# A linear-attention layer with its feed-forward part: rotary and decay products moved between engines and memories

## What is computed

```python
q = rope(norm(x) @ wq.T)            # 16 heads
k, v = rope(norm(x) @ wk.T), norm(x) @ wv.T     # 4 heads, each for 4 query heads
rot = jnp.concatenate([-x2, x1], axis=-1)       # rope: x * cos + rot * sin
scores = einsum('bhid,bhjd->bhij', q, k) * diag # diag: exp(-lam * (i - j)) for i >= j, else 0
o = einsum('bhij,bhje->bhie', scores, v)        # the chunked scan of the reference gives this sum
x = x + o @ wo.T
hidden = fwht(silu(norm(x) @ W1.T) * (norm(x) @ W3.T))
x = x + hidden @ W2.T
```

## Time and profile before

| | |
|---|---|
| median of 3 runs | 289.08 us (288.9 to 290.38) |
| profiled execution, first to last instruction (span) | 287.6 us |
| PE, VectorE (DVE), ACT, GpSimd (POOL) busy | 261.9, 229.2, 164.5, 175.0 us |
| share of the span | 91, 80, 57, 61% |
| DMA | 13.23 MB, 46 GB/s in the mean |
| chain that ended last | PE 34%, DVE 34%, POOL 13%, issue 12%, ACT 4% |

### The profile page before, as it was taken

How to read it: one execution, slowest core, us unless ns; L and a number is a source line. 1 busy time by engine, 2 the same in 40 slices (tenths; PEclk the granted TensorE clock), 3 DMA queues, 4 the chain that set the end, 5 groups by cost and what they waited for, 6 DMA issues and landing times.

```text
span 287.6 us, 4155 instructions
## 1 busy us (share of the span) xinstructions
PE 261.9 (91%) x1480; PEld 226.0 (79%) x1480; DVE 229.2 (80%) x324; ACT 164.5 (57%) x271; POOL 175.0 (61%) x117
## 2 busy tenths in 40 slices
PE   0897898997997999889999979969999999999995
PEld 0685677885896888778898878859888889988885
DVE  2878999999999999876989999999667686234323
ACT  2586776669475686556668658486445453033320
POOL 1049799789975978955687897969795610000000
PEclk9999999999999999999999999999999999999999
DMA  7694020211102020000001002200000000110002
GB/s 269 228 370 135 2 74 1 73 32 43 73 2 74 5 70 1 0 2 0 1 13 63 0 2 73 74 0 2 0 2 0 0 3 0 39 36 0 2 0 73
DMA packets 5203, 13.23 MB, mean 46 GB/s; under 512 B 576, under 2 KB 2112, under 8 KB 5184
## 3 DMA queue, kind: packets, MB, share of 16 engines
q1 hardware_dynamic: 4752, 12.65, 12.4%
q10 hardware_dynamic: 432, 0.33, 0.3%
HBM read 11.93 MB, written 1.05 MB: 45 GB/s over the span
## 4 chain that ended last, share of the span: by engine, by line
PE 34%; DVE 34%; POOL 13%; issue 12%; ACT 4%; DMA 1%; DVEq 0%; SPq 0%; POOLq 0%; ACTq 0%
PE bank L264 11%; PE bank L265 11%; PE bank L266 11%; DVE p_lo L780 7%; DVE rope_b L753 6%; POOL qk L629 6%; DVE p_raw L775 5%; DVE rope_a L752 5%; POOL q_hid L636 4%; DVE xn L721 3%; DVE w_lo L727 3%; DVE o_lo L785 2%; POOL k_lo L636 2%; ACT p_hi L507 1%; DMA x_sb<-in_x 1%
## 5 line engine op out<-in xcount | busy, mean ns | idle before, releaser
L629 POOL TENSOR_TENSOR qk<-rope_a,rope_b 128x512 f32<-128x512 f32 x40 | 66.9, 1687 | 18.9 <-DVE rope_b L753 18.8
L264 PE MATMUL bank<-xt_hi,w_hi 128*128 128x512 f32 x144 | 58.5, 407 | 5.2 <-DVE rope_a L752 3.8
L265 PE MATMUL bank<-xt_lo,w_hi 128*128 128x512 f32 x144 | 57.2, 397 | 0.0
L266 PE MATMUL bank<-xt_hi,w_lo 128*128 128x512 f32 x144 | 57.1, 397 | 0.0
L636 POOL TENSOR_TENSOR q_hid<-qk,q_hid 128x512 fp32r<-128x512 f32 x32 | 48.6, 1529 | 4.0 <-ACT q_hid L500 3.9
L780 DVE TENSOR_TENSOR p_lo<-p_raw,p_hi 128x512 fp32r<-128x512 f32 x32 | 40.1, 1255 | 3.0 <-ACT p_hi L507 2.6
L507 ACT ACTIVATE p_hi<-p_raw 128x512 fp32r<-128x512 f32 x48 | 30.1, 626 | 15.4 <-DVE p_raw L775 14.8
L264 PEld LDWEIGHTS bank<-xt_hi,w_hi 128*128 128x128 f32 x144 | 27.6, 192 | 13.5 <-DVE rope_a L752 5.5
L641 POOL TENSOR_TENSOR p_lo<-p_raw,p_hi 128x512 fp32r<-128x512 f32 x16 | 25.9, 1617 | 20.2 <-ACT p_hi L507 20.1
L753 DVE TENSOR_TENSOR rope_b<-rope_b,sin_sb 128x512 f32<-128x512 f32 x40 | 36.8, 919 | 0.0
L265 PE MATMUL bank<-w_lo,o_hi 128*128 128x256 f32 x128 | 36.2, 283 | 0.0
(11 more groups left out here) (70 smaller groups left out, 611.6 us busy)
## 6 DMA issues: line engine op xcount, KB each, us to landing
w_raw<-in_w SPq DMA_DIRECT2D x6, 512.0 KB, 3.2
w_raw<-in_wq SPq DMA_DIRECT2D x4, 512.0 KB, 4.8
decay_sb<-in_decay SPq DMA_DIRECT2D x4, 512.0 KB, 5.9
w_raw<-in_wo SPq DMA_DIRECT2D x4, 512.0 KB, 3.3
x_sb<-in_x SPq DMA_DIRECT2D x4, 256.0 KB, 4.6
out<-x_sb SPq DMA_DIRECT2D x8, 128.0 KB, 1.8
w_raw<-in_wk SPq DMA_DIRECT2D x1, 512.0 KB, 4.8
w_raw<-in_wv SPq DMA_DIRECT2D x1, 512.0 KB, 6.6
```

The costliest lines, as they stand in the source:

```text
L264: pe.matmul(o, a_hi, b_hi, start=first, stop=False, skip_group_check=shared)
L265: pe.matmul(o, a_hi, b_lo, start=False, stop=False, skip_group_check=shared)
L266: return pe.matmul(o, a_lo, b_hi, start=False, stop=last, skip_group_check=shared)
L629: pool.tensor_tensor(qk[:, r % 2, :], rope_a[:, r % 2, :], rope_b[:, r % 2, :], ALU.add).then_inc(rope_sum, 1)
```

## The change

The two swap copies on ACT are removed. VectorE makes the sine product straight from the projection's bank, in two operations on 64 partitions each, which read one half of the partitions and write the other; the cosine product comes third and frees the bank. The signs of the sine table move with the partitions that are read. The decay products of S_FIRST0 and S_SECOND are written back into their PSUM bank; ACT and VectorE read them there, and PE waits for the low part before it overwrites the bank. S_FIRST1 still goes through `p_raw`, now with a buffer per unit. The low parts of chunks 3 to 13 move from VectorE to GpSimd, at the end of each unit. The order is written anew on three engines: in unit u, ACT rounds the key ahead of `o_hi` of unit u - 1, and the first query ahead of `o_hi` of unit u; GpSimd adds and splits the key at the start and the queries in the unit that projects them; VectorE rotates the key after the first low part.

```diff
...
 x_hi_done, v_hi_done = sem("x_hi_done"), sem("v_hi_done")
-swapped, rope_parts, rope_sum = sem("swapped"), sem("rope_parts"), sem("rope_sum")
+sin_done, rope_sum = sem("sin_done"), sem("rope_sum")
 rope_hi, rope_lo = sem("rope_hi"), sem("rope_lo")
...
         pe.wait_ge(rope_lo, needed + 1)
-        if u:
-            pe.wait_ge(mask_done, 3 * (u - 1) + s + 1)
+        if u and s == S_FIRST1:
+            pe.wait_ge(mask_done, 3 * u)
+        elif u:
+            pe.wait_ge(p_lo_dve, 2 * (u - 1) + s + 1)
         if s == S_SECOND:
...
         g = p // PPG
-        if b == 0:
-            pe.wait_ge(p_lo_dve, 2 * (u + 1))
-        else:
+        pe.wait_ge(p_lo_dve, 2 * (u + 1))
+        if b:
             pe.wait_ge(p_lo_pool, u + 1)
...
         if n == 1:
-            pe.wait_ge(mask_done, 3 * UNITS - 1)
+            pe.wait_ge(p_lo_dve, 2 * UNITS)
         if n >= 2:
...
-    def swap(item):
-        n, r = LIN_NO[item], ROPE_NO[item]
-        act.wait_ge(lin_full, n + 1)
-        if r >= 2:
-            act.wait_ge(rope_sum, r - 1)
-        h = P // 2
-        act.activation(rope_b[0:h, r % 2, :], lin_bank(n)[h:P], ACT.Copy)
-        act.activation(rope_b[h:P, r % 2, :], lin_bank(n)[0:h], ACT.Copy).then_inc(swapped, 1)
     def high_rope(item):
...
             act.wait_ge(o_full, 2 * u)
-        act.activation(p_hi[:, s, :], p_raw[:, n % 2, :], ACT.Copy).then_inc(p_hi_done, 1)
+        src = p_raw[:, u % 2, :] if s == S_FIRST1 else s_bank[s][:]
+        act.activation(p_hi[:, s, :], src, ACT.Copy).then_inc(p_hi_done, 1)
     def high_o(u, b):
...
                     high_v(*item[1:])
-                else:
-                    swap(item)
...
     high_weights(2)
+    high_rope(("K", 0, 0))
+    high_v(0, 0)
+    high_rope(("Q", 0, 0))
+    high_v(0, 1)
     high_weights(3)
-    swap(("K", 0, 0))
-    swap(("Q", 0, 0))
-    high_v(0, 0)
-    high_rope(("K", 0, 0))
-    swap(("Q", 0, 1))
-    high_v(0, 1)
-    high_rope(("Q", 0, 0))
-    swap(("Q", 0, 2))
+    high_rope(("Q", 0, 1))
     high_v(0, 2)
-    high_rope(("Q", 0, 1))
-    swap(("Q", 0, 3))
+    high_rope(("Q", 0, 2))
     high_v(0, 3)
-    high_rope(("Q", 0, 2))
-    high_p(0, S_FIRST0)
     high_rope(("Q", 0, 3))
-    high_p(0, S_SECOND)
     for u in range(UNITS):
-        if u:
-            before = queries(u - 1)
-            fill(key(u - 1) + turned(u - 1))
-            for item in before[:1]:
-                high_rope(item)
-            high_p(u, S_FIRST0)
-            for item in before[1:]:
-                high_rope(item)
-            high_o(u - 1, 1)
-            high_p(u, S_SECOND)
-        fill(values(u)[:2] + queries(u)[:1])
+        fill(key(u - 1) + turned(u - 1) if u else [])
+        high_p(u, S_FIRST0)
+        high_p(u, S_SECOND)
         for item in key(u - 1) if u else []:
             high_rope(item)
-        fill(queries(u)[1:])
+        if u:
+            high_o(u - 1, 1)
+        fill(values(u)[:1])
         high_p(u, S_FIRST1)
+        fill(values(u)[1:2] + queries(u))
         if u in (UNITS - 2, UNITS - 1):
...
         fill(values(u)[2:3])
+        for item in queries(u)[:1]:
+            high_rope(item)
         high_o(u, 0)
+        for item in queries(u)[1:]:
+            high_rope(item)
         fill(values(u)[3:])
...
     def rope_add(item):
         r = ROPE_NO[item]
-        pool.wait_ge(rope_parts, r + 1)
+        pool.wait_ge(lin_free, LIN_NO[item] + 1)
         if r >= 2:
...
-    def low_p(u, s):
-        n = 3 * u + s
-        pool.wait_ge(p_hi_done, n + 1)
-        pool.tensor_tensor(p_lo[:, s, :], p_raw[:, n % 2, :], p_hi[:, s, :].bitcast(F32),
+    def low_weights(n):
+        _, _, at = CHUNKS[n]
+        pool.wait_ge(w_lo_done, n)
+        pool.wait_ge(w_hi_done, n + 1)
+        pool.tensor_tensor(w_lo[:, at:at + CH], w_raw[:, n % SLOTS, :], w_hi[:, at:at + CH].bitcast(F32),
+                           ALU.subtract).then_inc(w_lo_done, 1)
+    def low_p(u):
+        pool.wait_ge(p_hi_done, 3 * (u + 1))
+        pool.tensor_tensor(p_lo[:, S_FIRST1, :], p_raw[:, u % 2, :], p_hi[:, S_FIRST1, :].bitcast(F32),
                            ALU.subtract).then_inc(p_lo_pool, 1)
...
     def butterfly(dc, step):
...
     low_rope(("Q", 0, 0))
+    rope_add(("Q", 0, 2))
     low_rope(("Q", 0, 1))
-    rope_add(("Q", 0, 2))
     rope_add(("Q", 0, 3))
     low_rope(("Q", 0, 2))
+    low_weights(3)
     low_rope(("Q", 0, 3))
     for u in range(UNITS):
-        if u:
-            before = queries(u - 1)
-            for item in before[:1]:
-                low_rope(item)
-            if u % PAIRS == 3:
-                inverse_deviation(u // PAIRS + 1)
-            for item in key(u - 1):
-                rope_add(item)
-            for item in before[1:] + key(u - 1):
-                low_rope(item)
-        low_p(u, S_FIRST1)
+        before = key(u - 1) if u else []
+        for item in before:
+            rope_add(item)
+        if u % PAIRS == 3:
+            inverse_deviation(u // PAIRS + 1)
+        for item in before:
+            low_rope(item)
+        low_p(u)
         for item in queries(u):
             rope_add(item)
+        for item in queries(u):
+            low_rope(item)
+        if unit_chunk(u) is not None:
+            low_weights(unit_chunk(u))
         if u >= UNITS - 2:
...
     def rotate(item):
...
         n, r = LIN_NO[item], ROPE_NO[item]
-        dve.wait_ge(swapped, r + 1)
+        dve.wait_ge(lin_full, n + 1)
         if r >= 2:
...
                      for m in (lin_bank(n)[:], rope_a[:, r % 2, :], rope_b[:, r % 2, :]))
-        c, s = (tb[:].unsqueeze(1).broadcast_to([P, BH, SEQ]) for tb in (cos_sb, sin_sb))
-        dve.tensor_tensor(a, src, c, ALU.mult).then_inc(lin_free, 1)
-        dve.tensor_tensor(b, b, s, ALU.mult).then_inc(rope_parts, 1)
+        h = P // 2
+        for to, at in ((slice(0, h), slice(h, P)), (slice(h, P), slice(0, h))):
+            s = sin_sb[at, :].unsqueeze(1).broadcast_to([h, BH, SEQ])
+            dve.tensor_tensor(b[to], src[at], s, ALU.mult)
+        dve.tensor_tensor(a, src, cos_sb[:].unsqueeze(1).broadcast_to([P, BH, SEQ]),
+                          ALU.mult).then_inc(lin_free, 1)
     def mask(u, s):
         c, p = divmod(u, PAIRS)
...
             dve.wait_ge(decay_loaded[p // 2], 16)
-        if s == S_FIRST1:
-            dve.wait_ge(p_lo_dve, 2 * u + 1)
-        elif u and s == S_FIRST0:
-            dve.wait_ge(p_lo_dve, 2 * u)
-        elif u:
-            dve.wait_ge(p_lo_pool, u)
+        if s == S_FIRST1 and u >= 2:
+            dve.wait_ge(p_lo_pool, u - 1)
         table = decay_sb[:, 2 * p:2 * p + 2, :]
...
             src = s_bank[s][:].rearrange("p (b h t) -> p b h t", b=BH, h=2)
-            dst = p_raw[:, n % 2, :].rearrange("p (b h t) -> p b h t", b=BH, h=2)
         else:
             src = s_bank[s][:].rearrange("p (h t) -> p h t", h=2)
-            dst = p_raw[:, n % 2, :].rearrange("p (h t) -> p h t", h=2)
+        dst = p_raw[:, u % 2, :].rearrange("p (h t) -> p h t", h=2) if s == S_FIRST1 else src
         dve.tensor_tensor(dst, src, table, ALU.mult).then_inc(mask_done, 1)
...
     def low_p(u, s):
...
         dve.wait_ge(p_hi_done, n + 1)
-        dve.tensor_tensor(p_lo[:, s, :], p_raw[:, n % 2, :], p_hi[:, s, :].bitcast(F32),
+        dve.tensor_tensor(p_lo[:, s, :], s_bank[s][:], p_hi[:, s, :].bitcast(F32),
                           ALU.subtract).then_inc(p_lo_dve, 1)
...
     def low_o(u, b):
...
-    def fill(*lists):
-        for items in lists:
-            for item in items:
-                if item[0] == "X":
-                    low_x(*item[1:])
-                elif item[0] == "V":
-                    low_v(*item[1:])
-                else:
-                    rotate(item)
+    def fill(items):
+        for item in items:
+            if item[0] == "X":
+                low_x(*item[1:])
+            elif item[0] == "V":
+                low_v(*item[1:])
+            else:
+                rotate(item)
...
     dve.wait_ge(tables_loaded, 48)
-    fill(START[2:5])
-    low_weights(3)
-    fill(START[5:])
-    mask(0, S_FIRST0)
-    mask(0, S_SECOND)
-    low_p(0, S_FIRST0)
-    low_p(0, S_SECOND)
+    fill(START[2:])
     for u in range(UNITS):
+        before = key(u - 1) if u else []
+        mask(u, S_FIRST0)
+        mask(u, S_SECOND)
+        low_p(u, S_FIRST0)
+        fill(before + turned(u - 1) if u else [])
+        low_p(u, S_SECOND)
         if u:
-            mask(u, S_FIRST0)
-            mask(u, S_SECOND)
-            fill(key(u - 1) + turned(u - 1))
-            low_p(u, S_FIRST0)
             low_o(u - 1, 1)
-            low_p(u, S_SECOND)
         fill(values(u)[:1])
...
             add_attention(0, 1)
-        fill(values(u)[1:2] + queries(u))
+        fill(values(u)[1:2])
+        fill(queries(u))
         if u in (UNITS - 2, UNITS - 1):
...
         fill(values(u)[3:])
-        if unit_chunk(u) is not None:
-            low_weights(unit_chunk(u))
         i, p = u // PAIRS + 1, u % PAIRS
...
```

(2 more changed lines are left out.)

## The result

The changed kernel takes **313.11 us** (median of four runs, 311.73 to 314.31) against 289.24 for the kernel before in the same session: a ratio of 1.0809, with a 95% interval of 1.0776 to 1.0842. The ratio is the one on record; the quotient of the two medians is 1.0825. Ratios and their intervals leave out executions in the chip's slower state, which only e13 has, in two of six, the profiled one among them. The forecast was 310.0 in a range of 289 to 318. The profiled execution spans 311.2 us, where the one before spans 287.6.

What follows compares the result with a forecast made beforehand. VectorE and PE were taken as full in the first attention units, but the time as set by queue order. 289.1 - 0.6 - 14.1 + 36.5 = 310.9, less some 0.9 for p_hi copies, gave 310; range 289 to 318.

Steps and rivals of the forecast that it cites:

- The walk: Unit-by-unit schedule of all engine queues, giving each unit's first scores and PE waits summing to 40.2 us.
- The halved price: VectorE's sine operations on 64 partitions: 0.34 us each if halved, set aside for a full 0.68.
- VectorE's sum: VectorE's busy time over the kernel: from 229.2 to 211 us after sine, decay and chunk changes.
- Turned x: Units 5 and 13: transposes need both query banks free; PE waits 3.3 and 3.2 us.
- The four k_lo waits: PE's waits on the key's low part, expected to go as its add and low part come first on GpSimd.
- I take 36.5 as what is added: PE's added waits between first scores of units 0 and 14: 36.5 us, taken from the walk's 40.2.
- 36.5 - 14.1 - 0.9: Added PE waits 36.5, less 14.1 us of old waits and late steps, less 0.9 for cheaper p_hi copies.
- the sums win: Rival: VectorE's 18 us and GpSimd's freedom absorb the handoffs; 275 to 281, up to 287.6 us; chance 0.15.
- Shorter rotations: Rival: VectorE's rotations take 1.88 us, with other waits shorter; 291 to 302 us; chance 0.17.
- GpSimd's chunk at 3.4: Part of the worse case: chunk low part 0.9 us later in six units; 314 to 321; above 318, chance 0.05.
- the time is set by order: Main case, across the engines' queues: longer handoffs form a serial chain; 302 to 318 us, chance 0.56.
- three handoffs: Expected longer: key unit's rounding before o_hi and o_lo, chunk low part last on GpSimd, turned x's query banks.

Runs made afterwards that it cites:

- e13: The kernel before with two decay products in PSUM and low parts of chunks 4, 6 and 8 to 13 on GpSimd: 284.42 us, 0.9816.
- e10: The changed kernel with 12 useless matmuls issued ahead of each of the three chunk waits, so PE does not idle: 311.77 us, 1.0828.
- e4: The kernel before with only two of a unit's three decay products written back into PSUM and read there: 282.55 us, 0.9798.
- e1: The changed kernel with two items of ACT's queue exchanged, o_hi of the last unit ahead of the key's rounding: 299.3 us, 1.034.
- e4 to e6: e4, e6 and, between them, the kernel before with only the crosswise sine products instead of the swaps: 301.45 us, 1.0431.
- e6: The kernel before with only the low parts of chunks 3 to 13 on GpSimd, behind the queries' adds: 298.86 us, 1.0352.
- e9: The changed kernel with o_hi ahead of roundings, and the chunk's rounding and low part moved earlier on ACT and GpSimd: 297.38 us, 1.0299.
- e8: The kernel before with both the two decay products in PSUM and the crosswise sine products, chunks and order as before: 295.77 us, 1.0223.
- e12: The kernel before with all three decay products in PSUM, their low parts on VectorE, chunks 4, 6, 8 to 13 on GpSimd: 281.4 us, 0.9728.

## Why the prediction was right, and where its working was not

- **The total and the sign.** 310.0 forecast, 313.11 measured. Between the first scores of unit 0 and those of unit 14 the changed kernel needs 218.93 - 26.73 = 192.2 us, against 166.96 before: 25.2 more. The walk had unit 0 at 27.1 and unit 14 at 217.0. On the way it had unit 3 at 66.0 (67.44), unit 5 at 92.9 (95.29), unit 7 at 122.0 (123.82) and unit 11 at 174.6 (177.97), each a little early.
- **Prices.** A rotation, forecast at 2.1, is 42.74 to 44.84 = 2.10. Its three products step by 0.70 to 0.71, and the next, ordinary one by 0.61. By the rule of the Trainium skill ("VectorE: DVE Perf Modes", section "Two Vector instructions with no wait between them") none of the three may overlap the one before it: the trace agrees. The halved price that I set aside for 64 partitions is refuted (0.688). The PSUM write was taken at 0.60 a step and lasts 0.690, the same as other VectorE operations here. The decay low part at 0.68 (0.687), GpSimd's add at 1.29 (1.288), ACT's sum of 117 (116.3) and GpSimd's chunk of 2.5 (2.393) were right.
- **VectorE's sum** was mis-sized: 211 forecast, 218.6 measured. The step "40 x (1.36-0.919)" counts durations, while a busy time counts an overlap of 0.08 once. The sine product taken off had stood for some 0.84, and the operation ahead of a rotation is no longer overlapped by it: 80 x 0.08 = 6.4 us. The 120 products last 0.69 and not 0.68, another 1.2. These 7.6 us are an estimate, and as much as is missing. It had no part in the forecast time, which counted 2.1 a rotation.
- **The waits by kind.** o_lo: 11.2 forecast in six second attends, 10.1 measured in eight. Chunks: 3.1, 3.4 and 3.4 forecast, 8.7 in three measured. Turned x: 6.5 forecast, 4.8 measured. Banks: 7.7 forecast, 5.4 measured. The four k_lo waits went, as forecast. With the share of v_hid behind the first scores, 0.5, this is 29.5 us measured where I added 36.5, and 12.0 before.
- **The step that failed** is "I take 36.5 as what is added": the waits are 7 smaller, and in their place stands PE busy time, of which the forecast has none. Between the two marks PE is idle 29.5 us and busy 162.7, where before it was idle 12.2 and busy 154.8: 17.3 more waiting and 7.9 more busy time, with six stretches at the 1.2 GHz level, make the 25.2. The forecast had 36.5 - 14.1 - 0.9 = 21.5 there. It had 0.6 won ahead of unit 0 (1.0 measured) and nothing after unit 14's first scores (0.6 won). That 310.0 came within 3.1 of 313.11 is in part luck: the waits that were booked too high stand for a slow clock that was left out. That the walk booked as waiting what PE spent working slowly is likely and not shown; e10 took three slow stretches away and between the marks 1.7 us.
- **The rivals.** That the sums win is refuted for the whole change: o_lo is late by the rows above. It holds for one part alone, the decay product (e4, -6.3 us), which I had not separated. Shorter rotations are refuted by the step of 0.70. GpSimd's chunk at 3.4 is refuted by 2.393. The forecast's reason, "the time is set by order", is shown for one of its three handoffs by e1 (14 us from one exchange). It is not the whole cause: by e4 to e6 the parts alone, in the old order, come to 16.9 of the 23.9 us, if they add, and e9, with the chunk's place mended too, gave only 2 us beyond e1. The crosswise product costs 12.9 in the old order, by the bank that it holds longer and by VectorE's fullness, which the forecast counted in one sum with the chain. How much is the one and how much the other was not separated; e8 does not do it either.
- **What stays open.** The 7 us beyond the parts' sum are a difference of medians; e1 takes off twice that, so the order can also cost less than the sum of its places. In which of its places the 7 us arise was not tried, nor an order in which neither o_hi nor p_hi waits behind a rounding.

## What to carry to other kernels

A copy on an engine with slack can be cheap: to save 46 us of such copies by longer work on the full engine, which also held a bank, cost 12.9 us here. Take instead what makes the full engine's work shorter and leaves its handoffs where they are (the decay product in PSUM). Before a piece of work is moved, ask when its reader wants it, and whether the engine that takes it has room: the chunks read late went to GpSimd at a gain in e12 and at none in e13. In each queue, put what another engine waits for ahead of what itself still waits (e1), and look at once for the next item held behind it (e9). And price a part alone in the old order, as in a new one undoing it can cost more than the part.

## What the runs showed of the hardware that was not expected

- VectorE operations on 64 partitions take the full time (0.688 against 0.692 for 128), and three held ones in a row step by 0.70 and not 0.68.
- A product written into the PSUM bank it reads is as cheap as any (0.690), and its reader, now with one input in PSUM, is no longer drawn out beside a busy GpSimd (1.255 to 0.682 in e4). With more work on GpSimd and both inputs in SBUF the same low part went up to 1.580 (e6).
- PE fell to the 1.2 GHz level after the three chunk waits of 2.72 to 3.03 us (0.61, 0.76 and 0.72 granted in the windows above). With twelve matmuls issued into each it stayed at 2.4 GHz behind all three, with little or no gain in time. In that run it fell behind a wait of 1.84 us on o_lo, behind which it had not fallen in the changed kernel until the chunk's wait.
- The profile puts a wait on a GpSimd result down to "issue" for PE when other semaphores stood in the same wait: what ended just before, on all engines, names it.
